# Two subtractions of a preparation stage go from VectorE to GpSimd in a one-core graph attention kernel

## The reference, cut to what matters

```python
w_m = (efeat @ W_msg + b_msg).reshape(E, in_f, -1)
w_a = (efeat @ W_attn + b_attn).reshape(E, in_f, -1)
h_src = feat[src][:, :, None]
e1 = w_m * h_src
e2 = w_a * h_src
seg_max = jax.ops.segment_max(e2, dst, num_segments=N)
ex = jnp.exp(e2 - seg_max[dst])
denom = jax.ops.segment_sum(ex, dst, num_segments=N)
attn = ex / denom[dst]
ft = jax.ops.segment_sum(e1 * attn, dst, num_segments=N)
return ft.sum(axis=1)
...
x = _layernorm(x + gnn(...), axis=-1)
```

## Time and profile before

| | |
|---|---|
| median of 3 runs | 1586.32 us (1585.37 to 1590.31) |
| profiled execution | 1589.19 us |
| its span, first to last instruction | 1587.4 us |
| mean granted TensorE clock | 0.972 |
| busy: VectorE (DVE), TensorE (PE) | 1484.1, 1288.6 us |
| busy: GpSimd (POOL), ScalarE (ACT) | 1042.2, 1037.9 us |

### The profile page before, as it was taken

The page is one execution under the profiler, slowest core; times in us unless marked ns, Lnnn a source line. Parts: engine busy times, 40 slices in busy tenths (PEclk is TensorE's granted clock), DMA queues, the critical chain, the costliest instruction groups (busy, mean ns, idle before and its releaser), DMA issues. The chain is left out here.

```text
span 1587.4 us, 20981 instructions
## 1 busy us (share of the span) xinstructions
PE 1288.6 (81%) x5657; PEld 669.6 (42%) x5657; DVE 1484.1 (93%) x1519; ACT 1037.9 (65%) x2091; POOL 1042.2 (66%) x878
## 2 busy tenths in 40 slices
PE   0003899999999999999999999999999999999920
PEld 0002444444444444444444444444444444554420
DVE  7716999999999999999999999999999999999858
ACT  1002677777777777677777777777777767766445
POOL 5777777777788888777777777788888820000063
PEclk9999899999999999999999999999999999999955
DMA  4314444444444444444455444444444433322152
GB/s 108 94 18 119 91 130 137 130 130 119 129 132 124 123 126 123 129 127 128 122 137 128 129 119 133 128 128 121 128 132 128 117 99 100 93 83 90 56 149 71
DMA packets 175997, 182.89 MB, mean 115 GB/s; under 512 B 48245, under 2 KB 131546, under 8 KB 175881
## 3 DMA queue, kind: packets, MB, share of 16 engines
q1 hardware_dynamic: 142217, 159.14, 32.2%
q0 software_dynamic: 33664, 22.42, 10.1%
HBM read 92.56 MB, written 88.73 MB: 114 GB/s over the span
## 5 line engine op out<-in xcount | busy, mean ns | idle before, releaser
L538 POOL DMA_INDIRECT split<-x_parts,edge_src x784 | 945.3, 1206 | 263.8 <-issue 234.5
L868 PE MATMUL bank_sum<-em,row_onehot 128*128 128x512 f32 x1744 | 845.6, 597 | 0.8 <-ACT sum_rows L710 0.8
L1106 DVE TENSOR_TENSOR em<-bank_prod,h_rows 128x1024 f32<-128x1024 f32 x440 | 513.4, 1204 | 10.9 <-PE bank_prod L856 9.2
L868 PEld LDWEIGHTS bank_sum<-em,row_onehot 128*128 128x128 f32 x1744 | 313.9, 190 | 200.5 <-issue 163.4
L856 PE MATMUL bank_prod<-w_rows,partsT 100*128 100x512 bf16 x880 | 268.8, 388 | 1.6 <-DVE em L1106 1.6
L1124 DVE TENSOR_TENSOR em<-em 128x1024 f32<-128x1024 f32 x220 | 265.9, 1209 | 2.3 <-ACT em L669 2.3
L1149 DVE TENSOR_TENSOR em<-em,bank_max 128x2048 f32<-128x2048 f32 x110 | 250.1, 2274 | 4.3 <-ACT node_max L701 4.2
L669 ACT ACTIVATE em<-em 128x2048 f32<-128x2048 f32 x110 | 210.7, 1916 | 0.9 <-DVE em L1149 0.9
L710 ACT COPY sum_rows<-bank_sum 128x512 f32<-128x512 f32 x218 | 127.8, 586 | 105.9 <-PE bank_sum L868 105.9
L677 ACT CAST partsT<-bank_t 96x512 bf16<-96x512 f32 x220 | 117.2, 583 | 114.1 <-PE bank_t L825 110.5
L856 PEld LDWEIGHTS bank_prod<-w_rows,partsT 100*128 100x128 bf16 x880 | 79.6, 100 | 188.2 <-issue 157.9
(11 more groups left out here) (194 smaller groups left out, 1195.5 us busy)
## 6 DMA issues: line engine op xcount, KB each, us to landing
sums<-sum_rows SPq DMA_DIRECT2D x110, 512.0 KB, 3.0
rec<-split_records SPq DMA_DIRECT2D x220, 144.0 KB
split_records<-split SPq DMA_DIRECT2D x97, 288.0 KB, 2.3
mask<-tile_table SPq DMA_DIRECT2D x110, 192.0 KB, 3.3
split<-x_parts,edge_src POOLq DMA_INDIRECT x784
rel<-tile_table SPq DMA_DIRECT2D x110, 64.0 KB, 3.0
edge_feat<-in_features SPq DMA_DIRECT2D x97, 64.0 KB
flag<-tile_table SPq DMA_DIRECT2D x110, 2.0 KB
```

The lines of the kernel that those rows point to most:

```text
L538: return nc.gpsimd.indirect_dma_start(out, None, src, bass.IndirectOffsetOnAxis(idx, 0))
L868: mm = nc.tensor.matmul(sums_bank(t, g)[:, :], row_onehot[:, t % RING, g, :], em[:, t % RING, s * GROUPS + g, :, :, :].rearrange("p i m o ...
L1106: V.tensor_tensor(em[:, v, 2 * j:2 * j + 2, :, :, :].rearrange("p s i m o -> p s i (m o)"), bank_prod[j % 2][:, :, :].rearrange("p s (i x) ...
```

## The change

The subtractions of prep tiles 4 to 97 (`rest1`) and 3 to 97 (`rest2`) leave VectorE's list. GpSimd does them in the list of its gathers: behind the eight gathers of prep tile `q` come `rest1(q - 1)` and `rest2(q - 2)`. The first three or four prep tiles' subtractions, ahead of the main loop, stay on VectorE. ScalarE's, TensorE's and SyncE's lists are as before.

```diff
@@ gpsimd
-            for q in range(2, PREP_FIRST):
+            def words_of(q, n, lo):
+
+                u = q % PREP_RING
+                whole = split16[0:n, u, :, :].rearrange("p b (s k) -> p b s k", s=SLOTS)
+                return whole[:, :, :, lo:lo + FEAT]
+
+            def rest1(q):
+                if not prep(q):
+                    return
+                u, n = q % PREP_RING, prep_rows(q)
+                pool.wait_ge(in_part1, q + 1)
+                pool.wait_ge(in_rest1, q)
+                nc.gpsimd.tensor_tensor(in_rest[0:n, u, :, :].rearrange("p (b s) k -> p b s k", b=2),
+                                        edge_feat[0:n, u, :].rearrange("p (b s k) -> p b s k", b=2, s=SLOTS),
+                                        words_of(q, n, 0), ALU.subtract).then_inc(in_rest1, 1)
+
+            def rest2(q):
+                if not prep(q):
+                    return
+                u, n = q % PREP_RING, prep_rows(q)
+                pool.wait_ge(in_part2, q + 1)
+                pool.wait_ge(in_rest2, q)
+                r = in_rest[0:n, u, :, :].rearrange("p (b s) k -> p b s k", b=2)
+                nc.gpsimd.tensor_tensor(r, r, words_of(q, n, 48), ALU.subtract).then_inc(in_rest2, 1)
+
+            for q in range(2, PREPS + 2):
                 gather_features(q)
-            for q in range(PREP_FIRST, PREPS):
-                gather_features(q)
+                if q - 1 >= PREP_FIRST:
+                    rest1(q - 1)
+                if q - 2 >= PREP_FIRST - 1:
+                    rest2(q - 2)
...
@@ vector
             for t in range(FIRST, LAST + 1):
-                q = t + LEAD
                 times_features(t + 1, 0)
...
                 shift(t)
-                rest1(q)
-                rest2(q - 1)
```

## The result

The changed kernel was timed four times: 1569.5, 1570.69, 1597.46 and 1608.43 us, a median of 1584.08; the kernel before took 1585.37 to 1590.31 beside it, a median of 1587.78. The times of the changed kernel form two groups. The ratio of the two shorter ones is 0.9893, with a 95% interval of 0.9866 to 0.9919: in such an execution the change makes the kernel about 1.1% faster. The two longer ones are slower than the kernel before. The medians of all launches differ by 0.2%, and with the six launches of e8 five of ten are short and five long, so on average nothing is gained. Experiments e8 to e12 ask where the longer times come from. The profiled execution took 1570.69 us, with a span of 1568.9.

What follows compares the result with a forecast made beforehand. VectorE bounded the kernel before, GpSimd's longer list would after: pair 1.2 plus stall 1.5 make 2.7 us per prep tile, 93 x 2.7 - 202 = +49 on 1589.2 is 1638, less 2.9 gives 1635 us; range 1585 to 1795.

Steps and rivals of the forecast that it cites:

- The bound: Main loop before the change: VectorE never waits and its list sets the pace, 12.24 us per tile.
- the breakpoint: On GpSimd's list: the change neither gains nor loses time at x = 2.17 us per prep tile.
- the formula: Following GpSimd's list to `part2(97)` on ScalarE, the time changes by 93 x - 202 us.
- x: On GpSimd's list, a pair of subtractions plus that prep tile's stall; taken as 2.7 us.
- GpSimd needs 12.2 us per prep tile: Before the change, GpSimd's gathers and stalls need on average as much per prep tile as VectorE needs per tile.
- a pair is 1.2: The two subtractions of a prep tile on GpSimd take 1.2 us, with bounds of 0.46 to 2.5.
- rival B: GpSimd keeps up if pair and stall take 1.84 us or less; VectorE paces at 11.84; 1570 us, chance 0.09.
- The stall: Time GpSimd's gathers lose per tile while VectorE runs its block of four; taken as 1.5 us, mean before 2.1.
- The late subtractions: GpSimd's subtractions, behind the next gathers, hold up ScalarE: `part2(4)` near 150 us, ScalarE waiting in most tiles.
- Rival A: VectorE's block of four holds a GpSimd gather to its end in every tile; 1812 us, chance 0.2.
- The narrow place in the first `weigh`: Where a gather must start to be held through VectorE's block of four, 0.56 us into that instruction.
- Rival C: GpSimd subtractions delay VectorE's block of four by up to 0.45 us twice a tile; about 1655 us, chance 0.03.

Runs made afterwards that it cites:

- e8: The changed kernel again with nothing edited: three runs of 1569.7 to 1572.63 us and three of 1608.27 to 1608.89 us.
- e12: Changed kernel, GpSimd's pair waiting for VectorE's smaller maximum from prep tile 14 on, VectorE keeping the subtractions of prep tiles 4 to 13: 1593.99 us.
- e1: Changed kernel with both main-loop subtractions left out on both engines: 1546.54 us, ratio 0.9725 to the kernel before.
- e2: Changed kernel with one more subtraction on GpSimd behind each pair, into a spare tile: 1644.1 us, ratio 1.0334 to the kernel before.
- e3: Changed kernel with three more subtractions on GpSimd behind each pair, into a spare tile: 1724.28 us, ratio 1.0837 to the kernel before.
- e11: Changed kernel, GpSimd's pair waiting for VectorE's smaller maximum from prep tile 14 on: 1603.26 us, ratio 1.0106 to the kernel before.
- e7: Changed kernel with pairs ahead of the gathers and VectorE keeping the subtractions of prep tiles 4 to 13: 1552.04 to 1590.5 us, median 1588.69.
- e5: Changed kernel with each pair ahead of the gathers of the same step: three runs of 1559.45 to 1561.72 us, four of 1587.34 to 1599.49.
- e9: Changed kernel with only the first subtraction on GpSimd, VectorE keeping the second: 1608.42 us, ratio 1.0137 to the kernel before.
- e10: Changed kernel with only the second subtraction on GpSimd, VectorE keeping the first: 1603.82 us, ratio 1.0115 to the kernel before.
- e4: Changed kernel with VectorE keeping the subtractions of prep tiles 4 to 21: 1555.41 to 1607.65 us, median 1589.23.
- e6: Changed kernel with VectorE's two maxima replaced by one reduction over the four slots: 1785.52 us, ratio 1.1233 to the kernel before.

## Why the prediction was wrong

- **The bound, the breakpoint and the formula** were right. VectorE's shorter list is worth 44 us (e1; 38 forecast), GpSimd has almost no room beside the pair (e2), and 93 x - 202 gives e2 and e3 to within 0.2 in x.
- **"GpSimd needs 12.2 us per prep tile"** was a misreading. That is what it took in the trace of before; its own terms add up to 10.0 + 2.1 = 12.1, and the 2.1 of stall is no need of GpSimd's. In e1 the same gathers keep a pace of 11.84.
- **The step that failed is the size of the pair**, "a pair is 1.2" of the part on GpSimd's longer list. It measured 0.70. I took each subtraction as 0.3 and a gap of 0.3 behind it; they take 0.44 but start 0.38 apart, and 0.16 follow the second. With 1.2 and any stall over 0.64 GpSimd had to pace; with 0.70 and the 1.14 of the profiled execution x is 1.84. That is to the hundredth the point up to which rival B was said to hold, and not by chance: where VectorE paces, the stall fills its period.
- **The stall**, the other mis-sized term, was treated as a price that doesn't depend on who paces. 1.5 was right where GpSimd paces (1.5 in e2, 1.6 in e3, about 1.4 in e11), and too high in the profiled execution, where VectorE paces and one gather is held. With the pair at 0.70 and this stall x is 2.2 and the change about +3 us, so the two states lie less than 0.4 us of x apart. The pair's size takes 93 x 0.5 = 46 us off the forecast and the stall 33 more; some 12 of these are not had. The formula follows GpSimd's list, whose last gather ends at 1241.1, but `part2(97)` comes at 1253.63, in its turn on ScalarE's list, which here follows VectorE's pace.
- **The late subtractions** were half right. The start is late as worked out for B: `part2(4)` at 148.69 (150 forecast) and `part2(7)` at 182.54 (182.3). That the second agrees so well is luck: beside the 70 us of free gathers the sum had 4.2 of subtractions and nothing else, and the trace has three pairs of 0.70 and 2.3 of held gathers. In the loop ScalarE waits in most tiles only when GpSimd paces (e2, e11).
- **Rival A** did not come. The longest gather of the changed kernel's loop is 2 us. Why the kernel before had 40 gathers of over 4 us is open; no profiled execution of the changed kernel or of the twelve experiments had one. The narrow place in the first `weigh` that the prediction named is not enough for it: gathers that start 0.54 to 0.58 us into the first `weigh` take 1.45 to 1.50 in e2, e7, e11 and e12.
- **Rival B** came in the shorter executions, with its time. Its chance of 0.09 was too low: the subtraction's bounds of 0.46 to 2.5 for the pair reached far below the break-even, and I took a value by giving each of two instructions that follow each other a gap of its own.
- **Rival C** was put at 0.03 because nothing in the trace showed it. Its mechanism is real, at 0.23 us twice a tile where up to 0.45 was the bound: shown in the profiled executions of e5, e8, e9 and e10, and the times of all five executions of e9 and of e10 go with it. In the profiled one of the longer executions it makes the time 1609 us and not 1570. The longer times lie inside the stated range, but by this mechanism: VectorE has no gap there, where the forecast had GpSimd pacing and VectorE idle in every tile.

What decides at the start of an execution whether the pair falls beside the block or behind it is not settled. Nor is it settled why e11, and e4 and e7 for a part of the loop, go at 12.2 to 12.3 us with two held gathers where 11.84 with one would fit.

## What to carry to other kernels

When an engine's list is close to another's, moving work between them isn't priced by the sum of durations: find what each instruction holds up on the other engine, and then where in the other's list it will stand. A stall that one loop causes in the other can be what the slower loop's period leaves over, so don't add it to the other's work as if it were needed. The gap behind an instruction depends on what stands beside it (0.30 behind a gather, 0.16 behind a subtraction, none between two subtractions here), so don't take one gap for all, and when two estimates lie on both sides of a break-even, give both sides real chances. A change that wins only in one alignment of two loops should be timed often enough to see the other.

## What the runs showed of the hardware

- A gather whose row numbers lie in SBUF, started while VectorE runs an instruction with two SBUF operands, ends 0.81 to 0.83 us after that instruction's end in all 180 cases of the changed kernel's profiled execution (706.09 behind 705.27; 818.87 behind 818.04 in e6). The 40 gathers of over 4 us in the kernel before are an exception, held over four instructions. Beside a reduction of one operand a gather is not held.
- It goes both ways: a GpSimd subtraction of 0.44 us takes 1.41 when it meets a `weigh`, and a VectorE instruction with two SBUF operands that starts while a GpSimd subtraction runs takes 0.23 us more. The Trainium skill (SBUF — State Buffer, section Who interferes with whom) calls it an exclusive lock that whoever issues first keeps; the trace agrees in both directions, but for 0.06 us that the first `weigh` of e9 loses (1.27) to a subtraction that started after it.
- A GpSimd subtraction of 128 x 128 takes 0.44 us here, against 0.28 on VectorE; a reduction over four strided slots took 3.74 us for the 2048 elements per lane that two maxima handle in 1.22 + 0.68.
